# Routed networks of one Trainium2 kernel: spare weights and spare tables on two sets of semaphores

## What is computed

```python
def _fff(x, nw, nb, w1, b1, w2, b2, act):          # x: (8, 256, 128)
    node = zeros
    for _ in range(8):
        logit = einsum('bsd,bsd->bs', x, nw[node]) + nb[node]
        node = 2 * node + 1 + (logit > 0)
    leaf = node - 255
    h = act(einsum('bsd,bsdl->bsl', x, w1[leaf]) + b1[leaf])
    return einsum('bsl,bsld->bsd', h, w2[leaf]) + b2[leaf]
...
q, k, v = _fff(xn, q...), _fff(xn, k...), _fff(xn, v...)
y = xn + softmax(q @ k.T / sqrt(128)) @ v
out = y + _fff(y, f..., gelu)
```

## Time and profile before

| | |
|---|---|
| median of three runs | 2733.4 us (2726.75 to 2736.65) |
| the profiled execution | 2728.28 us |
| its span, first to last instruction | 2726.1 us |
| mean granted TensorE clock | 0.939 |
| TensorE matmul busy | 2392.7 us (88%) |
| VectorE busy | 1981.9 us (73%) |
| ScalarE busy | 1773.0 us (65%) |
| GpSimd busy | 1478.2 us (54%) |
| networks q, k, v, node products | 426 to 622 us of the span |
| network f, node products | 731 to 783 us of the span |

### The profile page before, as it was taken

One profiled execution on the slowest core, in us unless ns is written; L12 is line 12 of the kernel. 1 busy time (PEld: TensorE's weight loads), 2 busy tenths in 40 slices (PEclk: granted clock), 3 DMA queues, 4 the chain that ended last, 5 costly groups with the idle time before them and its releaser, 6 DMA issues.

```text
span 2726.1 us, 93471 instructions
## 1 busy us (share of the span) xinstructions
PE 2392.7 (88%) x35312; PEld 1684.3 (62%) x35340; DVE 1981.9 (73%) x3051; ACT 1773.0 (65%) x3674; POOL 1478.2 (54%) x1060
## 2 busy tenths in 40 slices
PE   7999867986475777768999999999999999999995
PEld 4777645665353344336777777777777777777774
DVE  5888654222324888867888888888888888888883
ACT  4666532333125677656887788878888788778873
POOL 2444314212212444546777777777777777777770
PEclk9999978988787989889999999999999999999996
DMA  9100015772231000001111212111211211121111
GB/s 333 47 0 0 1 31 152 226 219 63 69 101 63 1 0 0 0 17 33 31 46 46 54 31 54 47 45 32 62 39 37 63 47 31 31 72 44 31 31 32
DMA packets 143485, 153.91 MB, mean 56 GB/s; under 512 B 12272, under 2 KB 111920, under 8 KB 142256
## 3 DMA queue, kind: packets, MB, share of 16 engines
q1 hardware_dynamic: 139312, 144.53, 19.2%
q0 software_dynamic: 4096, 8.40, 1.1%
HBM read 75.29 MB, written 27.26 MB: 38 GB/s over the span
## 4 chain that ended last, share of the span: by engine, by line
PE 52%; issue 2%; PEld 1%; ACT 1%; DVE 0%; PEldq 0%; POOL 0%; POOLq 0%; DVEq 0%; ACTq 0%
PE ps L2028 12%; PE ps L2039 6%; PE ps L2071 6%; PE ps L2123 6%; PE ps L2092 5%; PE ps L2149 4%; PE ps L2060 4%; PE ps L2082 3%; PE ps L2158 3%; PE ps L2052 1%; PE ps L2138 1%; PE ps L2131 1%; ACT Y L1406 0%; PEld ps L2123 0%; ACT sq L2233 0%
## 5 line engine op out<-in xcount | busy, mean ns | idle before, releaser
L2426 POOL TENSOR_TENSOR c<-a,bq 128x1024 f32<-128x1024 f32 x192 | 454.6, 2368 | 239.8 <-DVE bq L2523 239.6
L2436 POOL TENSOR_TENSOR qn<-c,ss 128x1024 f32<-128x1024 f32 x192 | 378.5, 1971 | 28.4 <-issue 3.4
L2028 PE MATMUL ps<-wqk,xs 128*128 128x512 f32 x768 | 372.9, 609 | 14.2 <-POOL xs L2419 10.4
L2522 DVE TENSOR_TENSOR a<-ps,tab 128x512 f32<-128x512 f32 x384 | 263.0, 685 | 10.8 <-ACT sq L2233 5.6
L2523 DVE TENSOR_TENSOR bq<-ps,tab 128x512 f32<-128x512 f32 x384 | 261.5, 681 | 0.0
L2530 DVE TENSOR_REDUCE ss<-sq 128x16 f32<-128x1024 f32 x192 | 230.4, 1217 | 30.1 <-issue 16.2
L2444 POOL TENSOR_TENSOR z<-z,sm 128x1024 f32<-128x1024 f32 x96 | 182.8, 1904 | 118.1 <-DVE sm L2551 118.1
L1489 POOL TENSOR_TENSOR hC<-hs,Cs 128x1024 f32<-128x1024 f32 x64 | 150.4, 2355 | 177.6 <-ACT Cs L1641 90.9
L2233 ACT ACTIVATE sq<-ps 128x512 f32<-128x512 f32 x384 | 215.4, 597 | 36.3 <-PE ps L2028 36.2
L2028 PEld LDWEIGHTS ps<-wqk,xs 128*128 128x128 f32 x768 | 140.7, 193 | 139.9 <-issue 133.5
L2039 PEld LDWEIGHTS ps<-ident,qn 128*128 128x128 f32 x1536 | 175.9, 141 | 67.6 <-issue 47.4
(11 more groups left out here) (316 smaller groups left out, 5388.2 us busy)
## 6 DMA issues: line engine op xcount, KB each, us to landing
Vw<-Vs SPq DMA_DIRECT2D x192, 256.0 KB, 3.9
win_rows<-rows_q SPq DMA_DIRECT2D x24, 256.0 KB, 3.2
outs_q<-win_out SPq DMA_DIRECT2D x24, 256.0 KB, 3.1
wqk<-in_wqkv SPq DMA_DIRECT2D x6, 1024.0 KB, 5.0
leaves<-in_f_w SPq DMA_DIRECT2D x9, 576.0 KB, 4.5
leaves<-in_q_w SPq DMA_DIRECT2D x1, 4608.0 KB, 18.8
leaves<-in_k_w SPq DMA_DIRECT2D x1, 4608.0 KB, 22.4
leaves<-in_v_w SPq DMA_DIRECT2D x8, 576.0 KB, 4.4
```

The source lines that it names most:

```text
L2028: nc.tensor.matmul(jobs.out(n), xs[:, t * 128:(t + 1) * 128], wqk[:, (2 * y + s) * 512:(2 * y + s + 1) * 512], start=True, stop=True).then ...
L2426: nc.gpsimd.tensor_tensor(f(c), f(a), f(bq), ALU.add).then_inc(c_ready.sem, 1)
L2436: nc.gpsimd.tensor_tensor(qn[:, t, y, :, :, :].rearrange("p h s e -> p h (s e)"), c[:, y, :, :, :].rearrange("p h s e -> p h (s e)"), spre ...
L2522: nc.vector.tensor_tensor(a[:, y, :, s, :], Zs, spread(table(0, s), H1), ALU.mult)
```

## The change

The one semaphore of a group of spare windows becomes two. The four weight loads of a group count on `spare_w_in`, the four table loads on `spare_tab_in`. The node products (N) of a spare step wait for the weights alone, and the hidden products (H) of the same step, which TensorE reaches two steps later, get a new wait for the tables. No load is moved, added or taken out, and SyncE's order stays as it is. O comes behind H on TensorE and needs no wait of its own.

```diff
-        scattered, fetched, spare_in = [...], [...], [sem(f"spares_in{g}") for g in range(4)]
+        scattered, fetched = [sem(f"scattered{n}") for n in range(4)], [sem(f"fetched{n}") for n in range(4)]
+        spare_w_in, spare_tab_in = [sem(f"spare_w_in{g}") for g in range(4)], [sem(f"spare_tab_in{g}") for g in range(4)]
...
                     if i % 8 < 4:
                         row = sp.value_load(wrow[0:1, n, 4 * g + w:4 * g + w + 1])
-                        sp.dma_start(R.w[s][:, 4 * g + w, :], ...).then_inc(spare_in[g], 16)
+                        sp.dma_start(R.w[s][:, 4 * g + w, :], ...).then_inc(spare_w_in[g], 16)
                     else:
                         row = sp.value_load(trow[0:1, n, 4 * g + w:4 * g + w + 1])
-                        sp.dma_start(R.tab[s][32 * w:32 * w + 32, g, :], ...).then_inc(spare_in[g], 16)
+                        sp.dma_start(R.tab[s][32 * w:32 * w + 32, g, :], ...).then_inc(spare_tab_in[g], 16)
...
                         if g >= 8:
-                            pe.wait_ge(spare_in[g - 8], 16 * 8 * (n + 1))
+                            pe.wait_ge(spare_w_in[g - 8], 16 * 4 * (n + 1))
                         pe.wait_ge(x_ready, s + 1)
...
                     for s, n, g, at, wt, tab in stage(3):
+                        if g >= 8:
+                            pe.wait_ge(spare_tab_in[g - 8], 16 * 4 * (n + 1))
                         pe.wait_ge(oh_ready, s + 1)
```

More of the change, by code:

```diff
@@ L702, in routed0 @@
         chunk_ready, slot_ready, spare_ready = sem("chunks"), sem("slots"), sem("spares")
-        scattered, fetched, spare_in = [sem(f"scattered{n}") for n in range(4)], [sem(f"fetched{n}") for n in range(4)], [sem(f"spares_in{g}") for g in range(4)]
+        scattered, fetched = [sem(f"scattered{n}") for n in range(4)], [sem(f"fetched{n}") for n in range(4)]
+        spare_w_in, spare_tab_in = [sem(f"spare_w_in{g}") for g in range(4)], [sem(f"spare_tab_in{g}") for g in range(4)]
         win_in, win_out = [sem(f"win_in{j}") for j in range(NROWS)], [sem(f"win_out{j}") for j in range(NOUTS)]
@@ L783, in spare @@
                         row = sp.value_load(wrow[0:1, n, 4 * g + w:4 * g + w + 1])
-                        sp.dma_start(R.w[s][:, 4 * g + w, :], d[f"{NETS[n]}_w"][bass.ds(row, 128), :]).then_inc(spare_in[g], 16)
+                        sp.dma_start(R.w[s][:, 4 * g + w, :], d[f"{NETS[n]}_w"][bass.ds(row, 128), :]).then_inc(spare_w_in[g], 16)
                     else:
                         row = sp.value_load(trow[0:1, n, 4 * g + w:4 * g + w + 1])
-                        sp.dma_start(R.tab[s][32 * w:32 * w + 32, g, :], d[f"{NETS[n]}_tabr"][bass.ds(row, 32), :]).then_inc(spare_in[g], 16)
+                        sp.dma_start(R.tab[s][32 * w:32 * w + 32, g, :], d[f"{NETS[n]}_tabr"][bass.ds(row, 32), :]).then_inc(spare_tab_in[g], 16)
                 def renew(n, g):
```

## The result

The changed kernel's six runs gave a median of 2697.88 us (2688.76 to 2702.63), beside 2726.36 us for the kernel before over six runs (2721.72 to 2736.65). The ratio is 0.9886, with a 95% interval of 0.986 to 0.9912: 31 us less by the ratio, 28.5 by the medians, where 30.5 were forecast. The two later readings of the same kernel gave 0.9895 (0.9874 to 0.9917) and 0.9897 (0.9878 to 0.9915).

A forecast was written before the change was run, and what follows sets the result against it. TensorE, idle for late spare tables and then slowed by a low clock, was taken as the bound. Returns of 6.1, 10.3, 7.6 and 6.5 us sum to 30.5, so 2733.4 less 30.5 gives 2703 us, range 2692 to 2724.

The forecast's parts named there:

- What bounds the kernel: In the routed networks TensorE is the bound; its node products wait 19.1 us for spare tables, with slow clock behind.
- q, 6.1 us: End of network q: no wait remains and the clock stays up, so 3.4 of waiting and 2.7 of slow clock return.
- k, 10.3: Network k: of 13.35 us, 10.3 return; the first wait goes, 1.5 of waiting and 1.6 of slow clock remain.
- v, 7.6: End of network v: of 8.5 us of stall 7.6 return; a 0.9 us wait for weights remains without clock loss.
- the 2.2 us: Assumed time from issue to landing of a 144 KB spare weight load, with 2.0 and 4.4 as the ends.
- f, 6.5: End of network f: all 6.5 us return, 2.13 of waiting and an estimated 4.4 of slow clock.
- The new wait ahead of H costs nothing: TensorE's hidden products in spare steps: tables land before H, with a cover of 5 us in k and 4 in v.
- The slower rival: The new wait holds H in steps g = 8 to 11; tables some 14 us later would give 2747 or more; chance 0.03.
- The sixteen wait instructions cost nothing: The added waits on TensorE were costed at nothing, as N's sixteen present waits show no bracket of their own.
- The sum: Gains of the four routed networks: 6.1 (q), 10.3 (k), 7.6 (v) and 6.5 (f), together 30.5 us.
- Nothing changes: Rival: spare weights and tables land together if DMA engines work through a backlog, leaving 2733 us; chance 0.04.
- Weights land late: Rival: 144 KB weight loads take 4.4 us, all four networks still wait, only 10.1 us return, 2723; chance 0.13.

The follow-up runs named there:

- (3): The kernel before with the two sets of semaphores, both waited for ahead of N; medians 2714.43 and 2714.51 us, ratios 0.9979 and 0.9969 to the kernel before.
- (7): The changed kernel, but in network k alone the tables are waited for ahead of N as before; median 2700.95 us, ratio 0.9916 to the kernel before.
- experiment 6: The changed kernel with spare weights issued earlier and tables later in SyncE's order; medians 2686.81 and 2687.43 us, ratios 0.9878 and 0.9872 to the kernel before.
- (8): The changed kernel with the wait for tables one stage earlier, ahead of OH instead of H; one run, 2712.55 us.
- experiment 5: The kernel before with unused matmuls into PSUM bank 0 ahead of the six waits, keeping TensorE busy; median 2708.73 us, ratio 0.9957.
- (9): The changed kernel with the last four table loads of each network two SyncE steps later; median 2700.91 us, ratio 0.9914 to the kernel before.
- experiment 4: The kernel before with its one wait ahead of N written twice; median 2716.13 us, ratio 0.9977.

## Why the prediction was right

The forecast was 2703 us from a median of 2733.4; 2697.88 from 2726.36 is -28.5 by the medians and -31 by the ratio, against -30.5. Point by point:

- **What bounds the kernel.** Shown. With the wait put back (3) 0.2 and 0.3% are left of a gain of 1.0 to 1.1%, and one network put back (7) takes about its own share.
- **q, 6.1 us.** 6.1 in the trace. No wait in two of three traces of the change, 0.68 us in the third.
- **k, 10.3.** 11.3. Two errors cancel in part. The last weights landed about as forecast (issued at 534.9, used at 537.31, 2.4 us and not 2.2). But I let the first wait go altogether, and 0.56 to 0.75 us of it stayed, since the last weight of group 2 took 5.2 us to land (issued 525.74, used 530.92) and not 2.2. SyncE's timeline of the changed kernel shows what was issued ahead of it:

```profile
520.49 1.99 SPq L785 DMA_DIRECT2D leaves<-in_k_w  x3
522.53 1.15 SPq L651 DMA_DIRECT2D leaves<-in_v_w  x1
523.73 0.50 SPq L653 DMA_DIRECT2D leaftab<-in_v_tabp  x1
524.33 0.38 SPq L766 DMA_DIRECT2D win_rows<-rows_v  x1
524.75 0.51 SPq L774 DMA_DIRECT2D outs_k<-win_out  x1
525.74 0.36 SPq L785 DMA_DIRECT2D leaves<-in_k_w  x1
```

  Three weight loads, a renewed set's 704 KB, window rows and outputs, 1.6 MB in all, went to the queue in the 5 us ahead of that load. In the order of experiment 6, where it is issued earlier, the bracket is gone. That the backlog sets the landing is my reading of it; no run moved the renewed set alone. On the other side I charged 1.6 us of slow clock to the wait of 1.5 that remained, and behind the 1.36, 1.44 and 1.27 us that the three traces of the change show the clock stayed up.
- **v, 7.6.** 7.6: a wait of 0.85 us against 0.9 forecast, at full clock. One trace out of the variants (8) had 3.00 there, as the late weights would have it. So the 2.2 us is near the usual landing (2.6 us is the median of the 64 spare weight loads) and no bound.
- **f, 6.5.** 6.5 between the two first traces. But its larger term, 4.4 us of slow clock, is that of one execution. The second trace of before needs 41.88 us from the last node products to the mark (780.06 to 821.94), the first 44.94 (782.57 to 827.51), so 3.1 of the 4.4 are not always there. Against the 40.4 us of the change the first trace has 4.5 us of slow clock there, and the other four that wait for the tables ahead of N have 1.5 to 1.6: the usual size of this term is a third of the forecast's. The step "the slow clock behind the wait costs what this trace shows" was too sure for the other networks too: two traces of before differ by 5.3 us to the mark with nearly the same sum of waits. That the slow clock costs anything was right: experiment 5 returned 7 to 12 us by its traces and 11.7 by its times, with the caution there, where 13.7 were expected.
- **The new wait ahead of H costs nothing.** Right: no bracket on line 910 names a table. The cover in k was nearer 3.4 (8) or 4.3 us (9) than 5. The slower rival needs tables much later than any here; issued 6.5 us later in k, they cost 9.8 us in the trace and left the kernel 23 us under before (9).
- **The sixteen wait instructions cost nothing.** Not borne out, and with the other sign. With sixteen more waits ahead of N the time is 6 to 8 us less (3, 4). The change has sixteen more waits too, at another place, so some of its 31 us may come from this and not from the tables: between the kernel with both waits at N and the change the medians differ by 22 to 23 us. The traces (387.2 us to the mark on average for two of before, 359.1 for three of the change) give 28.1 to the routed part. How the two go together is open, and no experiment parted them for the wait ahead of H.
- **The sum.** That the 30.5 came within 2 us of the differences of the medians (28.5, 32.1 and 31.7) is in part luck. The waits and where they end were right; the slow clock was taken from the one trace of the kernel before that had more of it, k returned 1 us more than forecast, and an effect of 6 to 8 us that the sum has at nothing may be in what was measured.
- **The rivals.** Nothing changes: ruled out. Weights land late: not as this rival had it for all four networks, but single loads do take 4 to 5 us, as its row of 4.4 said; the median of the weight loads from issue to landing was 2.6 us, with 2.1 and 5.2 as the ends, in the trace after. The Trainium skill's 2 us of HBM latency at high load, which I had set beside it ("DMA: Bandwidth & Descriptors", Latency and other measured facts), would have left k waiting 3.3 us and v 2.7. The traces of the change have 1.27 to 1.44 and 0.49 to 1.27 us for the last weights, so as the usual landing it isn't borne out; whether it is what the single late loads met, no run here shows.

## What to carry to other kernels

When one semaphore counts several loads, ask of each consumer which of them it reads; on an engine with a fixed order a wait belongs ahead of the first instruction that needs the data, and with two semaphores the loads can then be ordered by who needs them first (here that second step was worth another 3 to 5 us). Price a stall on TensorE by the distance between like instructions around it, since the bracket leaves out the slow clock behind it, and take that part from more than one execution. Use a landmark inside the trace (here the last product of the routed networks) where an effect of a few microseconds is to be told from the spread of the rest.

## What the runs showed of the hardware that I had not expected

- With matmuls in place of idle time the granted clock stayed at 1.00 behind the waits and the kernel before became 0.43% faster while its loads were as late as ever (medians 2708.73 us against 2723.37); up to 6 us of it may be the unexplained effect of experiment 4.
- After waits of like length the clock stayed low for times that differed: 44.94 and 41.88 us from the last node products of f to the mark, in two executions of the same kernel. The weights' waits of 1.36, 1.44 and 1.27 us in k cost no clock, where one of 1.72 had (0.76 and 0.72 over the 6.6 us behind it), and so had one of 1.90 in experiment 8 (0.72 over 6.2 us).
- A wait on TensorE written twice, the second on a count that has been reached, made the kernel 0.23% faster (0.10 to 0.36 by the interval), and a split one 0.21 and 0.31%. The traces show no place for it.
